# Five tile pairs of the fourth sweep's last rows, loaded early into rooms whose rows are done

## The reference, cut to what matters

```python
x = ln(x + L0(x, adj))        # (adj @ x + beta*x) / (rowsum(adj) + beta) @ kernel + bias
x = ln(x + L1(x, adj))        # three times  h = relu(adj @ (h @ W) + b), widths 20, 20, 128; then relu(h + x)
x = ln(x + L2(x, adj))        # D^-1/2 adj D^-1/2 @ (x @ W + b)
x = ln(x + L3(x, adj))        # adj @ x + gamma * softmax(xWl (xWr)^T) x Wh Wg
```

## Time and profile before

| | |
|---|---|
| median of three runs | 1342.76 us (1340.31 to 1343.25) |
| profiled execution: time, span | 1341.3 us, 1339.5 us |
| TensorE matmuls busy | 1285.0 us (96%), 5911 instructions |
| VectorE busy | 930.6 us (69%) |
| ScalarE busy | 715.7 us (53%) |
| queue q1, moved | 286.30 MB, 57.2% of 16 engines' span |
| mean granted TensorE clock | 0.994 of 2.4 GHz |

### The profile page before, as it was taken

One profiled execution on the slowest core, in us unless ns is written; L12 is line 12 of the kernel. 1 busy time (PEld: TensorE's weight loads), 2 busy tenths in 40 slices (PEclk: granted clock), 3 DMA queues, 4 the chain that ended last, 5 costly groups with the idle time before them and its releaser, 6 DMA issues.

```text
span 1339.5 us, 17278 instructions
## 1 busy us (share of the span) xinstructions
PE 1285.0 (96%) x5911; PEld 792.2 (59%) x5911; DVE 930.6 (69%) x1207; ACT 715.7 (53%) x880; POOL 267.5 (20%) x175
## 2 busy tenths in 40 slices
PE   8999999999999899999999999998899999999987
PEld 3544444433232233778787788886677767767764
DVE  6666665551010365999999989896888788788885
ACT  1111111011110123688787877776788788788795
POOL 0111110010000010011111100005234334354345
PEclk9999999998999999999999999999999999999999
DMA  9886665555999899899999999970000000000000
GB/s 367 314 316 251 251 219 204 173 188 181 382 333 400 309 352 407 307 353 374 351 371 359 376 356 361 382 291 0 1 0 1 1 1 1 1 18 14 1 1 32
DMA packets 81087, 288.01 MB, mean 215 GB/s; under 512 B 9466, under 2 KB 11130, under 8 KB 81018
## 3 DMA queue, kind: packets, MB, share of 16 engines
q1 hardware_dynamic: 78768, 286.30, 57.2%
q10 hardware_dynamic: 2250, 0.82, 0.2%
HBM read 284.98 MB, written 2.10 MB: 214 GB/s over the span
## 4 chain that ended last, share of the span: by engine, by line
PE 79%; DVE 8%; ACT 4%; issue 4%; DMA 3%; POOL 1%; POOLq 0%; ACTq 0%; DVEq 0%; SPq 0%
PE acc L1298 17%; PE acc L1536 7%; PE acc L1454 7%; PE acc L1388 7%; PE acc L1449 6%; PE acc L1450 6%; DMA raw<-in_adj_s 3%; DVE t_lo L1029 2%; PE rs L1306 2%; PE acc L1526 2%; PE acc L1527 2%; PE acc L1530 2%; PE e L1491 2%; PE e L1493 2%; PE rs L1491 2%
## 5 line engine op out<-in xcount | busy, mean ns | idle before, releaser
L1029 DVE TENSOR_TENSOR t_lo<-raw,t_hi 128x1024 fp32r<-128x1024 f32 x256 | 311.1, 1259 | 26.7 <-ACT t_hi L743 21.8
L743 ACT ACTIVATE t_hi<-raw 128x1024 fp32r<-128x1024 f32 x256 | 261.5, 1054 | 40.5 <-PE acc L1454 39.9
L1449 PE MATMUL acc<-t_hi,st_hi 128*128 128x512 f32 x512 | 201.9, 394 | 0.9 <-ACT t_hi L743 0.9
L1450 PE MATMUL acc<-t_hi,st_lo 128*128 128x512 f32 x512 | 199.5, 390 | 0.0
L613 POOL TENSOR_TENSOR ring_lo<-ring,p_hi 128x1024 fp32r<-128x1024 f32 x64 | 155.4, 2429 | 220.0 <-ACT p_hi L799 219.9
L1298 PE MATMUL acc<-raw,x 128*128 128x512 f32 x400 | 179.3, 597 | 0.0
L1454 PE MATMUL acc<-t_lo,st_hi 128*128 128x512 f32 x512 | 159.5, 393 | 5.8 <-DVE t_lo L1029 5.0
L1103 DVE TENSOR_TENSOR ring<-ring,e 128x1024 f32<-128x1024 f32 x128 | 154.0, 1212 | 0.1
L793 ACT ACTIVATE ring<-ring 128x1024 f32<-128x1024 f32 x128 | 134.2, 1054 | 25.0 <-DVE ring L1103 24.9
L1298 PEld LDWEIGHTS acc<-raw,x 128*128 128x128 f32 x400 | 73.7, 190 | 92.0 <-issue 92.0
L1536 PE MATMUL acc<-ring,x 128*128 128x512 f32 x256 | 120.2, 592 | 0.0
(11 more groups left out here) (220 smaller groups left out, 1878.8 us busy)
## 6 DMA issues: line engine op xcount, KB each, us to landing
raw<-in_adj_s SPq DMA_DIRECT2D x506, 512.0 KB, 5.7
kept_t<-in_adj_s SPq DMA_DIRECT2D x8, 512.0 KB, 6.6
x<-in_x SPq DMA_DIRECT2D x4, 512.0 KB, 10.3
kept_x<-in_adj_s SPq DMA_DIRECT2D x4, 512.0 KB, 6.4
kept_e<-in_adj_s SPq DMA_DIRECT2D x4, 512.0 KB, 7.7
kept_l<-in_adj_s SPq DMA_DIRECT2D x4, 512.0 KB, 6.5
kept_s<-in_adj_s SPq DMA_DIRECT2D x4, 512.0 KB, 6.7
kept_v<-in_adj_s SPq DMA_DIRECT2D x4, 512.0 KB, 6.9
```

The source lines that it names most:

```text
L743: nc.scalar.activation(t_hi[:, g % HL, :], raw[:, k, :], ACT.Copy).then_inc(hi_done, 1)
L1029: nc.vector.tensor_tensor(t_lo[:, k, :], raw[:, slot_no(s, c, g), :], t_hi[:, k, :].bitcast(F32), ALU.subtract).then_inc(lo_done, 1)
L1449: mm(a[:, :], block_of(st_h, b), hi[:, m], start=(g == 0 and j == 0), stop=False)
L1450: mm(a[:, :], block_of(st_l, b), hi[:, m], start=False, stop=False)
```

## The change

Sweep 3 gets a second kind of held tile. Five pairs of its last three rows, (row, d) = (2, 4), (2, 5), (1, 3), (1, 4) and (0, 2), no longer go through the ring. Each is loaded into half of a room (or, for `kept_t`, a quarter) whose own row was done earlier in the sweep, after position 0, 1, 2, 3 and 3. SP issues a pair behind the first ring tile whose predecessor in the slot lies in a later position than the one that frees the room, which is behind ring tile 204, 206, 210 and, twice, 216. Each pair has a semaphore, on which TensorE waits. The order of the products is the same. The ring tiles of sweep 3 are now 196 to 239, at positions 5, 6 and 7 six, eight and ten of them, and `T_WIDE` is 240. The functions `order_of`, `wait_ring` and the wide sweeps are as before; their numbers follow.

```diff
@@ -65,6 +65,8 @@
 AHEAD = (1, 2, 2)
 LATE = 1
 FILL = {0: (0, 1), 2: (2, 3)}
+AHEAD_3 = ((2, 4), (2, 5), (1, 3), (1, 4), (0, 2))
+ROOM_FREE = (0, 1, 2, 3, 3)
 KEPT = tuple((c, c + 1) if c + 1 < NC else (c, c - 1) for c in range(NC))
 
 Item = namedtuple("Item", "d h kept fused seq")
@@ -87,7 +89,7 @@
 
 def held(s, c, d):
 
-    return d in KEPT[c] and not (s == 0 and c == LATE)
+    return d in KEPT[c] and not (s == 0 and c == LATE) or s == 3 and (c, d) in AHEAD_3
 
 
 def order_of(s, c):
@@ -268,6 +270,7 @@
         st_hi_done, st_lo_done = sem("st_hi_done"), sem("st_lo_done")
         st5_hi_done, st5_lo_done = sem("st5_hi_done"), sem("st5_lo_done")
         late_in = sem("late_in")
+        ahead_in = [sem(f"ahead_in{n}") for n in range(len(AHEAD_3))]
         S = {k: sem(f"s_{k}") for k in STAGES}
         (wt_mm, wt_done, wt_mean, wt_scaled, wt_centred, qk_mm, qk_done, q_mm, q_hi_done,
          q_lo_done, k_hi_done, k_lo_done, v1_done, vh_done, vl_done, s_mm, s_copied, s_maxed,
@@ -360,8 +363,12 @@
             else:
                 eng.wait_ge(pe_acc, row_end(s, r))
 
-        def kept_tile(c, d, h):
-
+        def kept_tile(s, c, d, h):
+
+            if s == 3 and (c, d) in AHEAD_3:
+                n = AHEAD_3.index((c, d))
+                region, base = ((kept_v, 0), (kept_s, 0), (kept_l, 0), (kept_t, 0), (kept_t, 2))[n]
+                return region[:, base + h, :]
             n = 2 * KEPT[c].index(d) + h
             region, base = {7: (kept_v, 0), 6: (kept_s, 0), 5: (kept_l, 0), 4: (kept_t, 0), 3: (kept_t, 4),
                             2: (kept_e, 0), 1: (kept_late, 0), 0: (kept_x, 0)}[c]
@@ -369,11 +376,14 @@
 
         def tile_of(s, r, i):
 
-            return kept_tile(row(s, r), i.d, i.h) if i.kept else raw[:, i.seq % RAW, :]
+            return kept_tile(s, row(s, r), i.d, i.h) if i.kept else raw[:, i.seq % RAW, :]
 
         def wait_tile(eng, s, r, i):
 
             c = row(s, r)
+            if s == 3 and (c, i.d) in AHEAD_3:
+                eng.wait_ge(ahead_in[AHEAD_3.index((c, i.d))], 32)
+                return
             if not i.kept:
                 eng.wait_ge(raw_in[i.seq % RAW], 16 * (i.seq // RAW + 1))
             elif s == 0 and c == 0:
@@ -485,13 +495,22 @@
                     sp.wait_ge(res_in, 64 * (c - 2))
                 for d in KEPT[c]:
                     for h in range(2):
-                        sp.dma_start(kept_tile(c, d, h), tile(c, 2 * d + h)).then_inc(res_in, 16)
+                        sp.dma_start(kept_tile(0, c, d, h), tile(c, 2 * d + h)).then_inc(res_in, 16)
 
             def load_late():
                 sp.wait_ge(pe_acc, NC)
                 for d in KEPT[LATE]:
                     for h in range(2):
-                        sp.dma_start(kept_tile(LATE, d, h), tile(LATE, 2 * d + h)).then_inc(late_in, 16)
+                        sp.dma_start(kept_tile(0, LATE, d, h), tile(LATE, 2 * d + h)).then_inc(late_in, 16)
+
+            def load_ahead(n):
+                c, d = AHEAD_3[n]
+                wait_row(sp, 3, ROOM_FREE[n])
+                for h in range(2):
+                    sp.dma_start(kept_tile(3, c, d, h), tile(c, 2 * d + h)).then_inc(ahead_in[n], 16)
+
+            row_of = {i.seq: (s, r) for (s, r), here in ITEMS.items() for i in here if not i.kept}
+            to_load = list(range(len(AHEAD_3)))
 
             def flat(s, r):
                 c = row(s, r)
@@ -505,12 +524,14 @@
                                      cols(x_dram, part_no, NB * D // XP)).then_inc(x_in[part_no], 16)
                     if i.kept:
                         if s == 0 and c == 0:
-                            sp.dma_start(kept_tile(c, i.d, i.h), tile(c, g)).then_inc(row0_in[g], 16)
+                            sp.dma_start(kept_tile(s, c, i.d, i.h), tile(c, g)).then_inc(row0_in[g], 16)
                         continue
                     if i.seq == first_of_1 + RAW:
                         load_late()
                     wait_ring(sp, i.seq)
                     sp.dma_start(raw[:, i.seq % RAW, :], tile(c, g)).then_inc(raw_in[i.seq % RAW], 16)
+                    while to_load and i.seq >= RAW and row_of[i.seq - RAW] > (3, ROOM_FREE[to_load[0]]):
+                        load_ahead(to_load.pop(0))
 
             first_of_1 = min(i.seq for r in range(NC) for i in ITEMS[1, r] if not i.kept)
 
@@ -1336,7 +1357,7 @@
                 for d in FILL[c]:
                     wait_h(pe, 0, d)
                     for b in range(CB):
-                        t = kept_tile(c, d, b // GB)
+                        t = kept_tile(0, c, d, b // GB)
                         m = mm(o[32 * b:32 * b + H, :], h_a[:, (d * CB + b) * H:(d * CB + b + 1) * H],
                                t[:, b % GB * CW:(b % GB + 1) * CW], start=(d == FILL[c][0]), stop=(d == FILL[c][-1]))
                 m.then_inc(fill_mm, 1)
```

## The result

The change makes the kernel slower. Twenty runs of each gave a median of 1346.91 us (1342.05 to 1348.31) after and 1341.14 us (1338.35 to 1344.23) before: ratio 1.0040, 95% interval 1.0032 to 1.0048. The forecast was 1341.3 us with a range of 1339.0 to 1343.9 us; it was worked out from a median before of 1342.76 us in three runs, so as a ratio it says 0.9989. The measured time lies above the range. The profiled execution has a span of 1345.3 us, 5.8 more than before. L1212, L1245, L1261 and L1388 are L1233, L1266, L1282 and L1409 in it, and one line further down in e2, e6 and e7.

What follows compares the result with a forecast made beforehand. Bound: saturated DMA late in the fourth sweep, just above an all-engine chain of 13.67 us per position. Gain 3.0 us less 1.5 for one clock fall: 1342.76 less 1.5 = 1341.3 us, range 1339.0 to 1343.9.

Steps and rivals of the forecast that it cites:

- Transfers: Ten tiles, 12.8 us of transfer, move from behind 487 us into idle queue time earlier in the sweep, at no cost.
- Cost nothing: Four tiles put ahead of ring tile 217, 5.1 us of transfers, delay nothing in position 5.
- The price given for cover gone: If ring tiles 217 to 221 lost their cover, each late tile costs up to 1.28 us.
- Rival E: Four tiles ahead of 217, or 238 and 239, come late in position 5 or 7; gain 0 to 1.3 us; chance 0.08.
- The chain's floor: Positions 5, 6 and 7 each hold a once-round-all-engines chain of 13.67 us without transfers; 3.0 us come back.
- the 0.2: Gain taken for position 6, out of 0 to 0.35 us.
- the pause of 0.51: Longer pause ahead of L955 in position 6, 0.51 us, which nothing in the change touches.
- The clock: Two new 2.5 us TensorE waits, positions 6 and 7; one fall to half clock likeliest, costing 1.5 us (0 to 3.6).
- rival C: Clock falls in both waits, positions 6 and 7, or stays down; up to 7.2 us, centre 1343.5, slower; chance 0.17.
- Even odds for each: Each new TensorE wait of 2.5 us, in positions 6 and 7, has about even odds of a clock fall.
- Rival D: Transfers alone set the sweep's end, so the whole 12.8 us comes off, 1330.0 us; chance 0.03.
- SP's stop at load_ahead(0): SP stands up to 3.5 us behind ring tile 204, holding tile 205; costs nothing, bounds 0 and 1.28 us.

Runs made afterwards that it cites:

- e2: The change with its last two pairs issued later, behind ring tiles 223 and 227 instead of both behind 216; median 1339.97 us, ratio 0.9994.
- e6: The change with only one of the last two pairs behind ring tile 216, the other behind 227; median 1340.83 us, ratio 0.9996.
- e7: The change with last two pairs behind tiles 223 and 227, plus unused matmuls in TensorE's waits of positions 2, 6 and 7; 1337.86 us, ratio 0.9976.
- e11: The change plus twelve unused matmuls ahead of the w3 product of position 2 only; median 1344.20 us, ratio 1.0019.
- e3: The change with only the last two pairs, (1, 4) and (0, 2), fetched ahead behind tile 216; median 1346.37 us, ratio 1.0037.
- e1: The change with only the first three pairs fetched ahead, without the four tiles behind tile 216; median 1340.20 us, ratio 0.9991.
- e8: The change plus unused matmuls in the waits of positions 2, 6 and 7 and ahead of position 5's second tile; 1340.70 us, ratio 0.9996.
- e9: The kernel before plus twelve unused matmuls ahead of the w3 product of position 2; median 1340.31 us, ratio 0.9991.
- e10: The change with position 5's w3 product done ahead of its first two tiles, loads unchanged; median 1341.57 us, ratio 1.0000.
- e4: The change plus ten unused matmuls ahead of the transpositions of positions 6 and 7; median 1344.27 us, ratio 1.0030.

## Why the prediction was wrong

**The step that failed** is in "Transfers": tiles 217 to 221 "are used from 487 us on", the ten tiles are "done by about 490; the transposition that follows the tenth tile of position 5 can't begin before ... 494.93 in any case. Cost nothing." Two things in it were wrong. It took the transposition as the first instruction that suffers, while the w3 product stands behind the second tile, 217, and was due at 487.5. And it began with an empty queue at 477. The two ring tiles issued just before took 7.0 and 7.9 us to land, and the four tiles came on top: by the reckoning tile 217 is in by about 485 and all ten by 490, but 217 landed at 490.57 and 221 at 495.7. So the term "Cost nothing" cost 2.4 us without any fall of the clock (e11: 11.67 less 9.29) and 5.1 in the change (14.42 less 9.29). The price given for cover gone, up to 1.28 us a tile, bounds it from above for four tiles (5.1). Rival E named this place, at 0.08, and let it only shrink the gain; it had no term for a position's start. Against it stood a freeing more than 6 us ahead of need, but tile 217 was issued 7.8 us ahead of need (478.57 to 486.35) and took 12.0. e3 shows that these four tiles, with the falls that come with them, alone give 1.0037.

**The chain's floor was right.** 13.67 us forecast, 13.69 or 13.70 found from 5 to 6 in e1, e2, e6, e7, e8 and e11. Position 7 won 1.53 (1.52 forecast) in e7 and e8. Position 6 won nothing of the 0.2: it takes 14.01 in all profiles without a fall, and e7 still has the pause of 0.51 ahead of its successor (L977), so the pause belongs to the position. What causes it stays open. The sum is 2.8 us, not 3.0, and e7 against e9 (0.9976 and 0.9991) is 0.15% (2.0 us), with intervals that overlap slightly.

**The clock.** The price was right, the number of places wrong. A fall behind one of the new waits cost 1.64 us (15.65 less 14.01), 1.5 forecast; in the executions profiled it fell behind position 6's wait in the change, e1, e2, e3 and e11, not in e6 and e10. But the change made a third, longer wait at tile 217, and there the fall takes the tile, the w3 product and what follows; and a fall at 460 us, where the queue had room before, now lengthened that wait. Together the clock makes 0.44% (1.0040 less 0.9996, 5.9 us), of which up to e9's 0.09% may have been there before as well. The twenty executions of the change say the same: the three fastest (1342.05 to 1342.88 us) have a mean granted clock of 0.991 or 0.992, the other seventeen (1344.61 to 1348.31) 0.986 to 0.990. The steps of the profiled execution add up to nearly as much. Lost are 2.38 us of lateness (e11), 1.90 of longer wait by the fall at 460 us (4.25 less 2.35), 0.85 for tile and product at half rate (the rest of 14.42 less 9.29), 1.61 for what is still at half rate in position 5 (15.31 less 13.70) and 1.64 for the fall behind 515 us, together 8.4. Won are 1.30 and 1.51. The net is 5.6 us, of 5.8 in the span. So rival C's sign came and its mechanism took part, but what started it is the late tile of rival E: without it the same two waits leave e2 at 0.9994, near the forecast's 0.9989. That exactly one of the change's two new waits was followed by a fall, as forecast, is partly luck: in e3 and e11 both were.

**How often it fell.** Behind the 3.0 us wait of position 6 the clock fell in five of the seven profiles that have it, behind the 2.65 us wait of position 7 in two of six (e3 and e11: transposition to w_l2 product 3.91 and 3.75 us, not 2.42), and behind the 3.34 us wait of position 2 in six of eight (not in the kernel before and e4). Even odds for each were fair. The Trainium skill (TensorE: Matmul & The Clock Gate, the section on the HAM clock gate) says that idleness halves the array's rate until sustained work lifts it; these traces agree in most cases and not in all.

**Rival D's** 12.8 us is out: none of the kernels without a late tile won more than 0.24%.

**SP's stop at load_ahead(0)** cost nothing, as forecast: e1 and e2 have it, 4 to 5 is 9.29 us in both, and from 445 to 545 us no tile releases TensorE.

## What to carry to other kernels

Judge a prefetch put into an in-order queue by the tile right behind it: what is still ahead of it in the queue, and the first instruction in the consumer's order that stands behind that tile, which may be an epilogue and not the tile's own product. When a transfer bound lies just above a chain, work the chain out first; here it left 2.8 of 12.8 us. A change that turns many short waits of TensorE into few long ones can have the clock as a cost of its own. Unused matmuls in the wait measure it, if they end before what is awaited; here they went with a faster kernel (e7 0.9976, e2 0.9994, intervals just overlapping).

## What the runs showed of the hardware

A wait of TensorE of about 3 us was followed by half the clock in most profiled executions but not in all: after waits of 3.34 us in six of eight, of 3.00 in five of seven, of 2.65 in two of six. In the waits for tile 217 it fell at 4.25, 2.98 and 2.79 us (the change, e3, e4) and not at 2.35 and 1.54 (e11, e6). At tile 217 in the change the clock was at half for 6.8 us in all. The kernel with all waits filled scatters less (e8: 1339.31 to 1342.04 us, the change 1342.05 to 1348.31). A fall of the matmul clock can cost transfer time: 56 GB/s over 10 us, as a ring's slots are let go later. Ten small fp32 matmuls in a wait delay nothing measurable when they end before what is awaited (e7's transposition starts 7.72 us behind the w3 product, as in e2). Twelve that ended 0.7 us after it (e8) did delay what followed.
